# Perceiver cross-attention and two blocks on one core: a main loop step with its last score behind the value products, clip bounds sent by transfer, and a rearranged start

## What is computed

```python
q = (query @ Wq + bq).reshape(B, Nq, H, D).transpose(0, 2, 1, 3)
k = (key_value @ Wk + bk).reshape(B, Nkv, H, D).transpose(0, 2, 1, 3)
v = (key_value @ Wv + bv).reshape(B, Nkv, H, D).transpose(0, 2, 1, 3)
attn = jnp.einsum('bhqd,bhkd->bhqk', q, k) * scale
attn = jnp.clip(attn, -CLAMP, CLAMP)          # CLAMP = 10000
attn = jax.nn.softmax(attn, axis=-1)
...
x = jnp.einsum('bhqk,bhkd->bqhd', attn, v).reshape(B, Nq, Cq)
return x @ Wo + bo
```

## Time and profile before

| what | value |
|---|---|
| median of 3 runs | 1136.06 us (1135.42 to 1138.60) |
| the profiled execution | 1140.12 us, span 1138.4 us |
| mean granted TensorE clock | 0.952 of full |
| PE busy | 1053.3 us (93%) |
| DVE busy | 810.1 us (71%) |
| ACT busy | 726.6 us (64%) |
| POOL busy | 380.4 us (33%) |
| transfers | 128.56 MB, 113 GB/s on average |

### The profile page before, as it was taken

One profiled execution on the slowest core, in us unless ns is written; L12 is line 12 of the kernel. 1 busy time (PEld: TensorE's weight loads), 2 busy tenths in 40 slices (PEclk: granted clock), 3 DMA queues, 4 the chain that ended last, 5 costly groups with the idle time before them and its releaser, 6 DMA issues.

```text
span 1138.4 us, 29247 instructions
## 1 busy us (share of the span) xinstructions
PE 1053.3 (93%) x11521; PEld 724.2 (64%) x11521; DVE 810.1 (71%) x1502; ACT 726.6 (64%) x1429; POOL 380.4 (33%) x440
## 2 busy tenths in 40 slices
PE   7899797999999999999999999999999888978997
PEld 6687475766667676676767676655555555646654
DVE  7466686878878888878888788877878123693553
ACT  2222486888878888877888887776767454404442
POOL 5633545444445444544444441030000000203320
PEclk9899698999999999999999999998989599998999
DMA  7754563555555554545545543223431000000001
GB/s 218 223 178 137 184 172 103 169 147 153 161 150 154 143 171 145 152 145 154 160 140 159 156 144 102 71 78 107 135 87 41 29 2 1 1 1 2 2 1 38
DMA packets 117138, 128.56 MB, mean 113 GB/s; under 512 B 20008, under 2 KB 91371, under 8 KB 116971
## 3 DMA queue, kind: packets, MB, share of 16 engines
q1 hardware_dynamic: 111498, 120.20, 36.1%
q10 hardware_dynamic: 5472, 6.23, 2.1%
HBM read 88.61 MB, written 37.75 MB: 111 GB/s over the span
## 4 chain that ended last, share of the span: by engine, by line
PE 82%; ACT 7%; DVE 6%; issue 2%; DMA 1%; POOL 1%; SPq 0%; ACTq 0%; POOLq 0%
PE acc L1783 23%; PE st L1743 17%; PE mx L1729 10%; PE kps L1691 9%; PE misc L1729 5%; DVE free_k L1425 2%; ACT prob L994 2%; PE st L1587 2%; ACT qst L906 2%; PE acc L1587 1%; PE setB L2042 1%; PE mx L1725 1%; ACT prob L1082 1%; PE st L1765 1%; PE mx L1582 1%
## 5 line engine op out<-in xcount | busy, mean ns | idle before, releaser
L1189 DVE TENSOR_REDUCE mxp<-mx 128x1 f32<-128x512 f32 x709 | 465.1, 683 | 121.7 <-PE mx L1729 86.9
L994 ACT ACTIVATE prob<-st 128x512 f32<-128x512 f32 x704 | 380.7, 600 | 146.0 <-PE st L1743 145.3
L1743 PE MATMUL st<-qst,kst 51*128 51x256 f32 x2048 | 414.1, 313 | 30.9 <-ACT qst L906 22.2
L1743 PEld LDWEIGHTS st<-qst,kst 51*128 51x128 f32 x2048 | 302.5, 193 | 66.7 <-ACT qst L906 25.4
L1729 PE MATMUL mx<-kst,qst 51*128 51x512 f32 x645 | 269.0, 438 | 1.7 <-DVE mxp L1189 1.5
L1189 DVE TENSOR_REDUCE mxp<-misc 128x1 f32<-128x512 f32 x315 | 215.0, 682 | 40.6 <-PE misc L1729 40.6
L994 ACT ACTIVATE xn<-st 128x512 f32<-128x512 f32 x320 | 173.7, 600 | 53.5 <-PE st L1743 53.2
L1783 PE MATMUL acc<-prob,v_raw 128*17 128x256 f32 x2816 | 194.5, 395 | 8.2 <-issue 5.2
L1729 PEld LDWEIGHTS mx<-kst,qst 51*128 51x128 f32 x645 | 123.3, 191 | 70.3 <-issue 35.8
L1729 PE MATMUL misc<-kst,qst 51*128 51x512 f32 x315 | 135.8, 431 | 0.0
L1691 PE MATMUL kps<-ctx_p,w_hi 64*128 64x256 f32 x528 | 129.5, 312 | 4.9 <-POOL ctx_p L717 4.9
(11 more groups left out here) (428 smaller groups left out, 1290.2 us busy)
## 6 DMA issues: line engine op xcount, KB each, us to landing
kst<-kscr SPq DMA_DIRECT2D x240, 128.0 KB, 2.5
kscr<-kraw SPq DMA_DIRECT2D x100, 256.0 KB, 2.7
kst<-kscr SPq DMA_DIRECT2D x240, 64.0 KB, 2.6
ctx<-in_ctxT SPq DMA_DIRECT2D x93, 128.0 KB, 2.6
ctx<-in_ctxT SPq DMA_DIRECT2D x184, 64.0 KB, 2.4
kscr<-prob SPq DMA_DIRECT2D x16, 256.0 KB, 4.6
kscr<-o_sb SPq DMA_DIRECT2D x12, 256.0 KB, 4.0
qscr<-v_raw SPq DMA_DIRECT2D x8, 256.0 KB, 2.5
```

The costliest lines, as they stand in the source:

```text
L994: act.activation(exps(unit_at(n)), st_bank("scores", unit_at(n))[:, :], ACT.Exp).then_inc(exp_done, 1)
L1189: dve.reduce_max(at, bank_of_max(n)[:, :], AX.X).then_inc(max_red, 1)
L1743: mm = pe.matmul(st_bank("scores", n)[:, h * T:(h + 1) * T], kst[row, j // 2, at:at + P], qst[row, 2 * (q % 3) + j // 2, :], start=True, s ...
```

## The change

- **Step.** A step now begins with both halves of the fourth score of the step before, paired with both halves of the first score of this step. Its first maximum stands behind these and one projection product. The score of unit n+1 stands last. Heads of the maxima are taken in the order 0, 2, 1, 3. The very last score is issued alone behind the loop, before the last value products.
- **ACT in a step.** The copy of the projection bank (keys or values) stands behind the first exponential of a step (t % 4 == 0), not behind the third; the accumulator is saved at t = 3. Shift rows are copied at t = 58 and have their place among the score banks there.
- **Low bound.** ACT makes it from the shift's columns (128 x 8) at t = 57; SP writes it to DRAM as a row and reads it back onto 128 partitions behind score 64 of a group. `spread_low`, its two matmuls and its two bank places are gone.
- **Start.** The 12 first maxima of group 1 use a second padded tile, qz2, set to zero by DVE and loaded by SP (`load_padded`, four transfers behind the last query projection). Three fillings stand to four maxima. DVE makes w_lo behind its last prologue reduction; POOL splits chunk (0, 0) before the keys of chunk 19. ACT copies chunk 19 before the first shift rows.
- **Biases.** One of the four additions in each of groups 1 to 4.

The diff, cut to its core (weights, semaphores' names and tiles left out):

```diff
@@ -332,11 +335,11 @@
 
         def fill(m):
 
-            return m - m // 6 + F0 if m % 6 < 5 else None
+            return m - m // 4 + F0 if m % 4 < 3 else None
 
         def after_fill(f):
 
-            return f - F0 + (f - F0) // 5 + 2
+            return f - F0 + (f - F0) // 3 + 2
 
         def bank_of_max(n):
 
...
@@ -370,7 +373,7 @@
 
         def head_of_max(m):
 
-            return (1, 0, 2, 3)[m % 4]
+            return (0, 2, 1, 3)[m % 4]
 
         def unit_at(n):
 
...
@@ -380,9 +383,7 @@
         for n in range(NU):
             q, t = n // UQ, n % UQ
             st_users.append(("scores", unit_at(n)))
-            if t == 3:
-                st_users += [("low", 2 * q), ("low", 2 * q + 1)]
-            if t == 59 and q + 1 < NQ:
+            if t == 58 and q + 1 < NQ:
                 st_users.append(("shift", q + 1))
         st_place = {user: place for place, user in enumerate(st_users)}
 
@@ -398,8 +399,6 @@
             user, m = st_users[place]
             if user == "scores":
                 eng.wait_ge(exp_done, unit_at(m) + 1)
-            elif user == "low":
-                eng.wait_ge(low_set, m + 1)
             else:
                 eng.wait_ge(shift_set, 2 * m + 2)
                 eng.wait_ge(flag_abs, m + 1)
...
+            def write_low(q):
+
+                sp.wait_ge(low_col, q + 1)
+                with nc.allow_non_contiguous_dma("1024 bounds from columns to a row"):
+                    sp.dma_start(lscr[q].rearrange("(j n p) -> p j n", j=4, n=QT), lowc[:, :, :]).then_inc(low_set, 16)
+
+            def read_low(q):
+
+                sp.wait_ge(low_set, 32 * q + 16)
+                wait(sp, clip_done, UQ * q)
+                sp.dma_start(low[:, :, :].rearrange("p j t -> p (j t)"),
+                             lscr[q].rearrange("(o n) -> o n", o=1).to_broadcast([P, 4 * T])).then_inc(low_set, 16)
 
             sp.dma_start(wk[:, 0, :], a["L0_xattn_Wk"][0:P, :]).then_inc(w_in, 16)
             load_early(0, 1, 0)
...
@@ -627,6 +654,8 @@
                     if 3 <= 8 * (q - 12) + k < 3 + len(wt):
                         name = list(wt)[8 * (q - 12) + k - 3]
                         sp.dma_start(wt[name], a[name].rearrange("(c p) n -> p c n", p=P)).then_inc(late_in, 16)
+                    if k == 7 and q + 1 < NQ:
+                        read_low(q + 1)
 
             for n in range(4):
                 if n % 2 == 0:
...
+                before = 3 + 2 * split_at[q, k]
                 pool.wait_ge(*(v_ctx_sem(c) if m else k_ctx_sem(c)))
-                pool.wait_ge(*((v_ps, v_steps(c)) if m else (k_ps, k_steps(c))))
+                pool.wait_ge(*((v_ps, v_steps(c)) if m else (k_ps, k_steps(c)) if c > KLEAD else (q_ps, B)))
                 pool.tensor_copy(hi, raw).then_inc(part_step, 1)
                 pool.wait_ge(part_step, before + 1)
                 pool.tensor_tensor(lo, raw, hi.bitcast(F32), ALU.subtract).then_inc(part_step, 1)
                 pool.wait_ge(part_step, before + 2)
 
-            for c in range(16, KLEAD):
+            for c in range(16, KLEAD - 1):
                 k_split(c)
-            pool.wait_ge(v_ps, VLEAD)
-            pool.wait_ge(k_ps, KLEAD)
-            for n, (raw, hi, lo) in enumerate(weights):
-                pool.tensor_tensor(lo, raw, hi.bitcast(F32), ALU.subtract).then_inc(part_step, 1)
-                pool.wait_ge(part_step, n + 4)
-            for k in range(2):
-                ctx_split(0, k)
+            ctx_split(0, 0)
+            k_split(KLEAD - 1)
+            ctx_split(0, 1)
             pool.memset(v4[:, 0:32, :, DH:VW], 1.0).then_inc(vcol_set, 1)
             pool.wait_ge(qscr_w, 256)
...
+                if 1 <= q <= 4:
                     pool.wait_ge(bo_in, 32)
-                    add_bias(0)
-                    pool.wait_ge(x_bias, 4)
+                    add_bias(0, (q - 1,))
+                    pool.wait_ge(x_bias, q)
                 if q == 12:
 
...
@@ -906,12 +929,12 @@
                     act.activation(qst[r:r + 3, at:at + 2, :], shift_bank(q)[r:r + 3, :].rearrange(
                         "p (i t) -> p i t", i=2), ACT.Copy).then_inc(shift_set, 1)
 
-            def low_bound(q, e):
-
-                act.wait_ge(low_ps, 2 * q + e + 1)
-                wait(act, clip_done, UQ * q)
-                act.activation(low_pairs[:, :, e, :], st_bank("low", 2 * q + e)[:, :].rearrange("p (i t) -> p i t", i=2),
-                               ACT.Exp, bias=negclip[:, :]).then_inc(low_set, 1)
+            def low_bound(q):
+
+                act.wait_ge(m_clip, 2 * q + 1)
+                wait(act, low_set, 32 * q)
+                act.activation(lowc[:, :, :], shift[:, :, :], ACT.Exp, bias=negclip[:, :],
+                               scale=-1.0).then_inc(low_col, 1)
 
             def save_acc(q):
 
...
@@ -992,19 +1015,18 @@
                 if n >= NX and n % 4 == 0:
                     act.wait_ge(pv_done, n // 4 - (2 if n < UQ * (NQ - 1) + 8 else 1))
                 act.activation(exps(unit_at(n)), st_bank("scores", unit_at(n))[:, :], ACT.Exp).then_inc(exp_done, 1)
-                if t == 3:
-                    for e in range(2):
-                        low_bound(q, e)
-                if t == 4 and q > 0:
+                if t == 3 and q > 0:
                     save_acc(q - 1)
-                if t % 4 == 2:
+                if t % 4 == 0:
                     c = k_job(q, t // 8)
                     if c is not None:
                         k_first_half(c, t % 8 // 4)
                     c = v_job(q, t // 8)
                     if c is not None:
                         v_copy_half(c, t % 8 // 4)
-                if t == 60 and q + 1 < NQ:
+                if t == 57 and q + 1 < NQ:
+                    low_bound(q + 1)
+                if t == 58 and q + 1 < NQ:
                     shift_rows(q + 1)
 
             def root(k, half):
...
@@ -1289,10 +1309,19 @@
                     dve.wait_ge(ln_rc, 2)
                     dve.tensor_scalar(xn[:, j, :], x_sb[:, j, :], mv[:, j, 0:1], rstd[:, j, 1:2],
                                       ALU.subtract, ALU.mult).then_inc(ln_xn, 1)
+                if m == after_fill(26 + 4 * 3) + 2:
+                    dve.wait_ge(xnT_ps, 4)
+                    dve.memset(qz2[:, 0:4, :].bitcast(F32), 0.0).then_inc(rows_set, 1)
                 for b in (1, 3):
                     if m == after_fill(26 + 4 * b):
                         turned_early(b)
                 shift_step(0, m - LD)
+
+            dve.wait_ge(part_step, 3)
+            dve.wait_ge(v_ps, VLEAD)
+            dve.wait_ge(k_ps, KLEAD)
+            for raw, hi, lo in weights:
+                dve.tensor_tensor(lo, raw, hi.bitcast(F32), ALU.subtract).then_inc(w_lo_set, 1)
 
             def add_norm(k, banks):
 
...
@@ -1714,15 +1744,15 @@
 
                 q, m = n // UQ, n % UQ
                 if m == 0:
-                    pe.wait_ge(qst_in, 64 * (q + 2))
+                    pe.wait_ge(qst_in, 64 * (q + 2 if q < 2 else q + 3))
                     if q > 2:
                         pe.wait_ge(zero_set, 2 + 2 * (q - 2))
                 if n % 8 == 0:
                     pe.wait_ge(*block_in(n // 8))
                 mx_free(pe, "max", n)
                 j, qt, at = head_of_max(m), m % 8 // 4, n // 8 % RB * 512
-                if n < UQ:
-                    pe.matmul(bank_of_max(n)[:, :], qz[:, j, qt * P:(qt + 1) * P], kst[:, j // 2, at:at + 512],
+                if n < AHEAD:
+                    pe.matmul(bank_of_max(n)[:, :], (qz, qz2)[q][:, j, qt * P:(qt + 1) * P], kst[:, j // 2, at:at + 512],
                               start=True, stop=True).then_inc(max_ps, 1)
                     return
                 row = slice(64 * (j % 2), 64 * (j % 2) + HR)
...
-
-                st_free(pe, "low", 2 * q + e)
-                row, at = slice(64 * e, 64 * e + HR), 2 * (q % 3)
-                pe.matmul(st_bank("low", 2 * q + e)[:, :], shrow[row, :],
-                          qst[row, at:at + 2, :].rearrange("p i t -> p (i t)"), start=True, stop=True,
-                          skip_group_check=True).then_inc(low_ps, 1)
 
             def values(q, k):
 
...
@@ -1894,34 +1916,32 @@
                 if t % 4 == 0:
                     some = passes(q, k, t % 8 // 4) if job(q, k) is not None else iter(())
                     more = n + AHEAD < NU
+                    if n:
+                        score_half(n - 1, 0)
+                    score_half(n, 0)
+                    if n:
+                        score_half(n - 1, 1)
+                    score_half(n, 1)
+                    next(some, None)
                     if more:
                         max_unit(n + AHEAD)
-                    score_half(n, 0)
-                    score_half(n, 1)
+                    next(some, None)
                     next(some, None)
                     if more:
                         max_unit(n + 1 + AHEAD)
                     next(some, None)
```

(26 more changed lines are left out.)

73 lines of the change are left out of this document (41 added, 32 removed).

## The result

The changed kernel takes 1354.19 us (median of 4 runs, 1348.96 to 1359.52) against 1135.74 us (4 runs of the kernel before beside it): a ratio of 1.1935, 95% interval 1.1859 to 1.2012. The direction was forecast, the size was not: 1162 us stood in the prediction, and 1354 lies 172 us above the end of its range. The profiled execution of the changed kernel took 1356.67 us, its span is 1354.9 us, and the granted clock fell from 0.952 to 0.911.

The account below looks back on a forecast made before the run. TensorE, 93% busy, was taken to bound the kernel through its order and waits. Terms 69 - 12 - 5 - 8 - 7 - 7 + 1 - 5 = +26 us on the 1136.06 us median gave 1162 us, range 1127 to 1182.

Parts of the forecast that it names:

- the 5 us a group that I named as the worst case: Low bound's write and read: two landings lost per group if loads ahead did not cover SP's wait; priced at 0.
- The turned step: Main loop, 237 steps: fourth maximum waits for the first's bank, mean step 3.18 us, +69 us in all.
- Rival C: Main loop: fourth maximum's bank is free in time, steps 2.90 us with projections, 2.64 without; 1084 us, 12%.
- Spreading gone, -12: Each group: the low bound's two spreading matmuls go, 0.73 us in 15 groups and 1.3 in the last.
- Step behind the turn, -5: Step behind the spreading: TensorE's 0.49 us wait is hidden by a longer step and fewer activations, 13 groups times 0.4.
- Group turn, -8: Group's turn: TensorE's wait for and turning of shift rows falls from 1.8 to 1.3 us, 15 times.
- the wait named as next: Group's turn: the score after the next waits for VectorE's flag reduction, behind a maximum that starts later; within the 1.3 us.
- Bias stall, -7: Second group: TensorE's 5.25 us stall behind POOL's four biases goes (-4.8), with the half clock behind it (1.9).
- Start, -7: Prologue: POOL splits a chunk earlier, so the loop starts sooner despite more maxima among fillings; between -5 and -8 us.
- The first product: End of the prologue: the loop's first projection product comes at about 123 us, not 128.30.
- The clock: After group turns: about half the half-clock stretches go with shorter waits, -5 us, between -10 and 0; new pauses cost 0.
- rival B: Most groups: the clock falls, 15 groups lose 1.5 us each and the 5 us don't come back; 1180 us, 15%.

Follow-up runs that it names:

- a_on_best: The turned step laid out anew around both bank waits, in the changed kernel with its low bound made on the chip: 1126.97 us, ratio 0.987.
- best1: Kernel before plus the turned step laid out anew, biases in group 13, POOL's memsets inside the branch's arms, bound on chip: 1110.78 us, ratio 0.974.
- best2: best1 with the low bound sent through DRAM in rows of 32 bytes in place of the spreading matmuls: 1093.92 us, ratio 0.960.

## Why the prediction was right in direction and 192 us off in size

**The step that failed** is one sentence: "The bounds now go through 16 small writes and 16 broadcast reads on SP's queue ... so I price this at 0. Without that cover a group would lose two landings, 5 us." I costed the write by the landing of loads of 64 KB and asked only whether SP's wait for it is covered. Both were the wrong question. The write is 1024 packets of 4 bytes into 4 KB; it landed after 10 us; and its cost fell on transfers that have nothing to do with it, of which one, POOL's code behind its branch, was on no list of mine. Intervals 16 and 1 of the 15 groups cost 140.5 us more with it than with 32-byte rows (264.2 against 123.7 in the table), and intervals 2 to 12 another 16 (541.7 against 525.7). These 16 lie in two groups: half-clock steps at the start of group 12, and in group 14 a wait of 5.27 us for keys with half clock behind it. The medians say 159 us (1354.2 against 1195.5). No rival had it. The range had no room for it either: the 5 us a group that I named as the worst case, 75 in all, were left out of it, and they were the landings of large transfers, no bound for a form that the trace didn't show.

**The turned step: right.** 237 times 0.29 to 0.32 us were forecast, +69 in all. In the undisturbed form, intervals 2 to 12 cost 49.4 us in 165 steps, 0.30 each. Each time within the step was met within 0.05 us, and the test of the cause (first maximum first) gave the time back. Rival C, in which the turn works, is refuted for this order. Its free bank is what a_on_best then built by hand, but with steps of 2.87 us in both kinds, not 2.64 without projections.

**Missed beside it: 8 of the 12 us in the 13th interval.** The other four are the turned step's own 0.3 in each of 15. VectorE's seven small operations of the shift stand there between reductions. In groups 0 to 10, where POOL works beside it, some of them take several times as long (last section), and the interval is 3.9 us; in groups 11 to 13, without POOL's work, it is 3.2, like any other step. So it is not the small operations that were missed but their wait for POOL. The kernel before has such a wait too, but VectorE had the slack for it.

**Spreading gone, -12: right in direction, -16, but given back.** Between the changed kernel with the bound on chip and with it in 32-byte rows the 15th interval falls by 16.3 us (64.9 to 48.6), but intervals 16 and 1 grow by 15.9 (107.8 to 123.7), 13 of them at the four group starts behind a bias. PE comes earlier and waits there. The profile puts these waits down to ScalarE in part; I put them down to POOL's release, because only with that release moved forward (best1 to best2) did part of the gain show. No run moves it in this kernel.

**Step behind the turn, -5: right for the turned step alone.** The wait falls into the 16th interval. Taken above the median step of its own kernel and summed over groups 1 to 13, it is 7.3 us before and 2.1 with the turn alone: the longer step hides it. I let ScalarE's part of the wait decide, but POOL's decides: moving POOL's release alone brings it to 1.6. In the changed kernel it is 3.3 with the bound on chip and 12.4 with 32-byte rows, both with biases ahead of the branch. **Group turn, -8: right, and a little more.** Taken the same way, the 14th interval was 1.83 us longer than a step and is now 1.05, where 1.8 and 1.3 were forecast: -10 in these 13 groups. The table's -9 for all 15 has the longer step in it. PE's waits for the shift rows, 22.2 us in the kernel before, are now 10.1 us for VectorE's flag, the wait named as next.

**Bias stall, -7: wrong**, 0 in a run of its own. The stall went as forecast; "fits into POOL's pauses" failed, since its pauses in front of a group's start are on the path.

**Start, -7: wrong, about +4.** In this pair of traces the first value products come 5.9 us later (141.0 against 135.1), over all traces of either start 4. The first product was near right: it came at 125.34 us and not at 123, since three weight subtractions on VectorE took 0.65, 1.48 and 1.09 us, not 3 x 0.68, and at 122.2 to 125.3 in the twelve kernels with this start. What failed is a second stall behind it, 9.5 us on PE, which I did not look for:

```profile
136.86 0.47 ACT L901 ACTIVATE kraw<-kps,bk 128x256 f32<-128x256 f32 x1 [14.14 <-DMA kscr<-o_sb]
```

That is ScalarE's first key copy, which overwrites keys that SP is still writing out. SP's queue is later by the padded tile's four loads, and the copy now stands ahead of three exponentials of its step and not one, so they wait too. I traced SP's chain up to the context load and not to its last writes.

**The clock: wrong sign.** -5 was forecast, and the granted clock fell from 0.952 to 0.911: a stretch at half clock now stands behind every stall. In the runs with the turned step and without the stall the granted clock is 0.966 to 0.986, above the 0.952 of before, in spite of the pauses in every step: rival B's reason did not appear.

## What to carry to other kernels

Don't scatter single 4-byte elements side by side into DRAM while anything else needs transfers: write what one partition holds as one run and turn the view where it is read; look for the transfer with the smallest element first, whatever its bytes. A gain in front of a group's start is worth nothing while another engine's release has no slack there, so find the last arrival at the place where the time is to be saved. And when a buffer rotates over n places, issue first what frees it latest.

## What the hardware did that I had not expected

- A write of 1 KB as 256 elements of 4 bytes delayed an instruction fetch on another queue by about 7 us, and 4 KB as 1024 elements delayed the landing of unrelated loads from some 2.5 to some 12 us. The same 1024 elements 64 bytes apart delayed the fetch by about 1 us.
- A branch over long code on POOL costs 2.5 to 3.6 us in groups 1 to 11 of the kernel before, once a group, and 11.7 to 13.5 in groups 2 to 11 of the changed kernel, behind the write.
- VectorE's operations on 128 x 8 values take 0.15 to 0.21 us, but while POOL works three of the seven take 0.61 to 0.86, and they end when POOL's ends. VectorE, then POOL, in a_on_best:

```profile
481.77 0.61 DVE L1208 TENSOR_SCALAR spad<-shift 128x8 bf16<-128x8 f32 x1
...
482.88 0.85 DVE L1211 SCALAR_TENSOR_TENSOR sres<-shift,spad 128x8 f32<-128x8 f32 x1
...
484.93 0.74 DVE L1220 TENSOR_TENSOR spad<-sres,spad 128x8 bf16<-128x8 f32 x1
```

```profile
481.73 0.61 POOL L677 CAST kraw<-kraw 128x512 fp32r<-128x512 f32 x1 [4.33 <-ACT kraw L886]
482.42 1.28 POOL L679 TENSOR_TENSOR kraw<-kraw 128x512 f32<-128x512 f32 x1
...
484.33 1.29 POOL L729 TENSOR_TENSOR ctx_p<-ctx,ctx_p 128x512 fp32r<-128x512 f32 x1
```

481.77 + 0.61 is 482.38, POOL's cast ends at 482.34; 482.88 + 0.85 is 483.73, POOL's subtraction ends at 483.70; the third end at 485.67 and 485.62. In the groups without POOL work (779 us in the same trace) the same operations take 0.16 to 0.19 us, and the 13th interval is 2.86 us in place of 3.94. The Trainium skill, "SBUF — State Buffer", section "SBUF: two separate sides", says that GpSimd and VectorE's operations of some forms (two inputs in SBUF, or a mode that uses two ports) take a shared port pair as an exclusive lock, held for the whole instruction; the end times agree. No run here took the lock away by itself.
